# Kernel of six chained blocks on one core: head of the first cross attention, written-out loops and job order of the second one

## The reference

```python
x = x + L0_xattn(layernorm(x), ctx, ctx, wq, bq, wk, bk, wv, bv, wo, bo)  # 16 heads of 8, keys: 1601
x = x + L0_attn(layernorm(x), W_KQV, W_O)                 # causal, rotary, 16 heads of 8
x = x + L0_ffn(layernorm(x), router_w, w1, w2)            # 8 experts, the best 2 used
x = x + L1_xattn(ctx, layernorm(x), ln1.., ln2.., Wq, Wkv, Wo)  # 16 heads of 64, keys: 1601 + 64
x = x + L1_attn(layernorm(x), time_decay, time_first, time_mix, Wk, Wv, Wr, Wo)
x = x + L1_ffn(layernorm(x), w1, b1, w2, b2)              # quantised piecewise-linear GELU
```

## Time and profile before

| | us |
|---|---|
| Median of 3 runs (1848.03 to 1851.46) | 1851.17 |
| The profiled execution, as a run | 1853.56 |
| Its span from first to last instruction | 1851.5 |
| Busy in it: TensorE matmuls (PE) | 1656.6 |
| weight loads (PEld) | 1374.1 |
| VectorE | 1276.0 |
| ScalarE | 959.0 |
| GpSimd | 603.7 |
| First cross attention | until about 570 |
| Second cross attention | about 765 to 1765 |

### The profile page before, as it was taken

One profiled execution on the slowest core, in us unless ns is written; L12 is line 12 of the kernel. 1 busy time (PEld: TensorE's weight loads), 2 busy tenths in 40 slices (PEclk: granted clock), 3 DMA queues, 4 the chain that ended last, 5 costly groups with the idle time before them and its releaser, 6 DMA issues. The chain is left out here.

```text
span 1851.5 us, 36685 instructions
## 1 busy us (share of the span) xinstructions
PE 1656.6 (89%) x13452; PEld 1374.1 (74%) x13452; DVE 1276.0 (69%) x2833; ACT 959.0 (52%) x1788; POOL 603.7 (33%) x855
## 2 busy tenths in 40 slices
PE   6999999999998898289999998999999989999965
PEld 3666666666666787278988888888888888898843
DVE  7666666666673776477777676777776767776577
ACT  3555555655553344155555465555554555556433
POOL 2000000000001221354455545553555455643110
PEclk8999999999998999699999999999999999999986
DMA  5533453535320011300000000000000000000000
GB/s 147 144 72 90 107 145 93 115 90 123 75 55 1 24 47 69 126 30 12 31 19 31 21 22 20 30 30 14 19 31 30 13 20 30 30 1 1 1 3 9
DMA packets 32711, 91.19 MB, mean 49 GB/s; under 512 B 8552, under 2 KB 17424, under 8 KB 32528
## 3 DMA queue, kind: packets, MB, share of 16 engines
q1 hardware_dynamic: 32384, 88.09, 17.7%
q10 hardware_dynamic: 144, 0.61, 0.2%
HBM read 40.43 MB, written 8.91 MB: 27 GB/s over the span
## 5 line engine op out<-in xcount | busy, mean ns | idle before, releaser
L385 DVE TENSOR_TENSOR c_p_lo<-c_turn_ps,c_p_hi 128x512 fp32r<-128x512 f32 x384 | 265.2, 691 | 214.1 <-ACT c_p_hi L334 200.0
L334 ACT ACTIVATE c_p_hi<-c_turn_ps 128x512 fp32r<-128x512 f32 x384 | 228.8, 596 | 296.7 <-PE c_turn_ps L242 292.6
L1006 DVE TENSOR_REDUCE a_chunk_max<-a_side_ps 128x1 f32<-128x512 f32 (+1 forms) x416 | 260.8, 665 | 111.8 <-PE a_side_ps L757 111.6
L376 DVE TENSOR_REDUCE c_chunk_max<-c_score_ps 128x1 f32<-128x1024 f32 (+2 forms) x384 | 262.2, 729 | 31.5 <-PE c_score_ps L272 30.9
L2326 PE MATMUL c_pv_ps<-c_p_hi,c_v_lo 128*128 128x256 f32 (+2 forms) x896 | 267.4, 298 | 0.0
L352 ACT ACTIVATE c_prob<-c_score_ps,c_neg_max 128x1024 f32<-128x1024 f32 (+1 forms) x256 | 245.5, 959 | 39.6 <-DVE c_neg_max L423 39.6
L242 PE MATMUL c_turn_ps<-consts,c_prob 128*128 128x128 f32 (+1 forms) x1792 | 248.7, 278 | 12.7 <-DVE c_p_lo L385 12.4
L2327 PE MATMUL c_pv_ps<-c_p_hi,c_v_hi 128*128 128x256 f32 (+2 forms) x896 | 249.7, 279 | 0.0
L2328 PE MATMUL c_pv_ps<-c_p_lo,c_v_hi 128*128 128x256 f32 (+2 forms) x896 | 249.2, 278 | 0.0
L914 ACT ACTIVATE a_prob<-a_st_ps 128x1024 f32<-128x1024 f32 (+1 forms) x224 | 214.4, 958 | 53.6 <-PE a_st_ps L741 53.6
L242 PEld LDWEIGHTS c_turn_ps<-consts,c_prob 128*128 128x128 f32 (+1 forms) x1792 | 197.4, 141 | 27.2 <-DVE c_p_lo L385 15.3
(11 more groups left out here) (334 smaller groups left out, 2780.5 us busy)
## 6 DMA issues: line engine op xcount, KB each, us to landing
a_stack<-a_k_hi SPq DMA_DIRECT2D x126, 200.1 KB, 4.2
a_stack<-a_k_lo SPq DMA_DIRECT2D x63, 200.1 KB, 4.2
a_ctx<-in_ctx_dram SPq DMA_DIRECT2D x16, 768.0 KB
c_ctx<-in_ctx_dram SPq DMA_DIRECT2D x16, 768.0 KB
absorbed_queries<-b_q_out SPq DMA_DIRECT2D x16, 512.0 KB, 3.5
c_q_raw<-absorbed_queries SPq DMA_DIRECT2D x16, 512.0 KB, 3.2
w<-in_L_ffn_w_dram SPq DMA_DIRECT2D x2, 512.0 KB
fold_raw<-in_L_xattn_Wkv_dram SPq DMA_DIRECT2D x2, 512.0 KB
```

The lines of the kernel that those rows point to most:

```text
L334: last = nc.scalar.activation(p_hi[u][:, 4 * c:4 * c + 4, P * j:P * j + P], turn_ps[c % 2][:].rearrange("p (t q) -> p t q", t=4), ACT.Copy)
L376: nc.vector.reduce_max(chunk_max[:, s % 2, c:c + 1], score_ps[:, maxima_of[c]], AX_X).then_inc(chunk_max_done, 1)
L385: last = nc.vector.tensor_tensor(p_lo[u][part], turn_ps[c % 2][:].rearrange("p (t q) -> p t q", t=4), p_hi[u][part].bitcast(F32), ALU.subt ...
L1006: nc.vector.reduce_max(out, rows, AX_X).then_inc(side_taken, 1)
```

## The change

It has four parts.

1. The `Fori` over passes 1 to 6 of `attend` becomes a Python loop on all five engines, so all eight passes are written out and their semaphore counts are constants.
2. In `attend`, ScalarE does a job "a" ahead of high halves 2 and 3 of its slot, and VectorE does the job "a" of the slot before ahead of low halves 2 and 3.
3. In the first cross attention VectorE splits the late queries an octet after the product: the high part in step 4 and the low part in step 5 of octets 2, 4, 6, 8.
4. In its head, SyncE issues all twelve stacking transfers of batch 0, the high parts as soon as the high keys are there, and ScalarE none. The second `take_turned` comes after the second of the four query splits. The masks of `wo_half` come after the first shift. The first six maxima of octet 1 leave `first_sides`; steps 0 to 3 of octet 0 now hold units 0 to 3, 4 to 7, 8 to 11 and 12.

```diff
@@ attend @@
-        for kind, ks in (("first", 0), ("mid", None)):
-            if ks is None:
-                with sp.Fori(1, BODIES - 1) as k:
-                    lay.sync_body(sp, k, kind)
-            else:
-                lay.sync_body(sp, ks, kind)
+        lay.sync_body(sp, 0, "first")
+        for k in range(1, BODIES - 1):
+            lay.sync_body(sp, k, "mid")
...
-        with pe.Fori(1, BODIES - 1) as k:
+        for k in range(1, BODIES - 1):
             body(k, "mid")
...
+                at(k, kind, s, "a")
                 if before:
                     high_halves(k, kind, s, 2)
                     high_halves(k, kind, s, 3)
-                at(k, kind, s, "a")
...
+                if s and (s - 1, "a") in table[kind]:
+                    lay.dve_take(dve, table[kind][s - 1, "a"], base(kind, k), k, kind, s - 1)
                 if s >= 2 or kind != "first":
                     low_halves(k, s - 1, 2)
                     low_halves(k, s - 1, 3)
                 maximum(k, s, 0)
-                if s and (s - 1, "a") in table[kind]:
-                    lay.dve_take(dve, table[kind][s - 1, "a"], base(kind, k), k, kind, s - 1)
                 maximum(k, s, 1)
@@ first cross attention @@
 def max_units_at(n, s):
+    if n == 0 and s <= 3:
+        return [("max", 1, i) for i in range(4 * s, min(4 * s + 4, UNITS))]
...
-    return [("max", 0, i) for i in range(UNITS)] + [("shift", 0)] + [("max", 1, i) for i in range(6)]
+    return [("max", 0, i) for i in range(UNITS)] + [("shift", 0)]
...
+            def stack_first_keys():
+                sp.wait_ge(k_high, CHUNKS)
+                sp.wait_ge(pads_set, 1)
+                for group in range(2):
+                    stack_part(0, group, 0)
+                    stack_part(0, group, 2)
+                wait_keys_done(sp, 0)
+                for group in range(2):
+                    stack_part(0, group, 1)
+                stack_keys(0, 1)
...
-            act.wait_ge(first_low[0], CHUNKS)
-            for i, part in enumerate((k_hi, k_lo, k_hi)):
-                nc.scalar.dma_start(stack[32 * i:32 * i + 32, 0, 1, 0:CTX].bitcast(F32), part[32:64, :].bitcast(F32)).then_inc(stacked[0], 16)
...
             for i in range(GROUPS):
                 dve.wait_ge(q_done, i + 1)
                 split_queries(i)
-            take_turned(1)
+                if i == 1:
+                    take_turned(1)
             dve.wait_ge(weights_loaded, N_WEIGHTS)
             nc.vector.tensor_copy(bv_wide[:], bv_rows[:].unsqueeze(2).broadcast_to([P, QUADS, P])).then_inc(bias_wide, 1)
-            for i in range(2):
-                nc.vector.tensor_scalar(g.wo_half[:, :, i, :], ...
...
             take_side(sides[UNITS])
+            for i in range(2):
+                nc.vector.tensor_scalar(g.wo_half[:, :, i, :], ...
...
-                    take_queries(job_at(n, s))
+                    if n in (2, 4, 6, 8) and s == 4:
+                        dve.wait_ge(job_taken, number["q", n // 2 - 1, 0] + 1)
+                        high_queries(GROUPS + n // 2 - 1)
+                    if n in (2, 4, 6, 8) and s == 5:
+                        low_queries(GROUPS + n // 2 - 1)
```

More of the change, by code:

```diff
@@ L215, in _ @@
         body(0, "first")
-        with pool.Fori(1, BODIES - 1) as k:
+        for k in range(1, BODIES - 1):
             body(k, "mid")
@@ L364, in _ @@
         body(0, "first")
-        with act.Fori(1, BODIES - 1) as k:
+        for k in range(1, BODIES - 1):
             body(k, "mid")
@@ L442, in _ @@
         body(0, "first")
-        with dve.Fori(1, BODIES - 1) as k:
+        for k in range(1, BODIES - 1):
             body(k, "mid")
@@ L639, in load_ctx, with stack_part @@
                              dram.ctx[b:b + 1, FULL * P:CTX, :].rearrange("o p d -> p (o d)")).then_inc(ctx_loaded, 16)
+            def stack_part(b, group, i):
+                part = (k_hi, k_lo, k_hi)[i]
+                sp.dma_start(stack[32 * i:32 * i + 32, b % 2, group, 0:CTX].bitcast(F32), part[32 * group:32 * group + 32, :].bitcast(F32)).then_inc(stacked[group // 2], 16)
             def stack_keys(b, u):
                 for group in (2 * u, 2 * u + 1):
-                    if b == 0 and group == 1:
-                        continue
-                    for i, part in enumerate((k_hi, k_lo, k_hi)):
-                        sp.dma_start(stack[32 * i:32 * i + 32, b % 2, group, 0:CTX].bitcast(F32), part[32 * group:32 * group + 32, :].bitcast(F32)).then_inc(stacked[u], 16)
+                    for i in range(3):
+                        stack_part(b, group, i)
+            def stack_first_keys():
[8 more added lines that the diff above has]
+                stack_keys(0, 1)
             sp.dma_start(g.x_tok[:], dram.x.rearrange("(t b) s d -> (b s) t d", b=2)).then_inc(loaded, 16)
@@ L670, in _ @@
                     load_ctx(b + 1)
+                if b == 0:
+                    stack_first_keys()
+                    continue
                 wait_keys_done(sp, b)
                 for u in range(QUADS):
-                    if b == 0 and u == 0:
-                        sp.wait_ge(pads_set, 1)
                     if b >= 2:
@@ L1030, in take_keys, with high_queries, low_queries @@
                                                ALU.add, ALU.subtract).then_inc(job_taken, 1)
-            def take_queries(job):
-                if not job or job[0] != "q":
-                    return
-                dve.wait_ge(job_taken, number[job] + 1)
-                split_queries(GROUPS + job[1])
+            def high_queries(i):
+                v, cols = i % GROUPS, slice(i // GROUPS * BANK, i // GROUPS * BANK + BANK)
+                nc.vector.tensor_copy(q_st[:, v, cols].bitcast(F32R), q_raw[i % 2][:]).then_inc(q_high, 1)
+            def low_queries(i):
+                v, cols = i % GROUPS, slice(i // GROUPS * BANK, i // GROUPS * BANK + BANK)
+                dve.wait_ge(q_high, i + 1)
+                nc.vector.tensor_tensor(q_st[64:ONES_AT, v, cols], q_raw[i % 2][64:ONES_AT], q_st[64:ONES_AT, v, cols],
+                                        ALU.subtract).then_inc(q_split, 1)
             def take_low_keys(b, c, bank):
@@ L1052, in split_queries @@
             def split_queries(i):
[L1053 to L1057 removed]
+                high_queries(i)
+                low_queries(i)
             sides = first_sides()
```

10 lines of the change are left out of this document (2 added, 8 removed).

## The result

| | before | after |
|---|---|---|
| Median, us | 1850.65 (4 runs, 1848.03 to 1851.46) | 1797.9 (4 runs, 1797.4 to 1799.11) |
| Ratio to before, 95% interval | | 0.9705 (0.9688 to 0.9723) |
| Profiled execution, us | 1853.56 | 1797.4 |
| Its span, us | 1851.5 | 1795.5 |

The change takes 52.75 us off the median.

The account below looks back on a forecast made before the run. TensorE, busy 1656.6 of 1851.5 us, was taken as the bound, so only its idle gaps and half-clock stretches could go: 26.4 + 17.4 + 7.1 + 6 = 56.9 us off 1851.2, giving 1794; own range 1786 to 1801, 8-in-10 range 1783 to 1809.

Parts of the forecast that it names:

- the list of signs: What would show the forecast in the profile, among it second-attention passes 115 to 116 us long instead of 122.8.
- (c): Second attention: the 3.6 us gaps are work at the turn of a pair and stay; 1820 us, chance 0.06.
- (d): Second attention: straight code waits at each block of code; gain eaten, or up to 1967 us, chance 0.03.
- rival (e): Full clock through the head, and register waits saved in six passes: 1786 us, at the edge of the forecast's 0.62.
- 20.6 - 1.4 = 19.2 us can go: Second attention: all TensorE waits on `c_x_lo` vanish except one of 1.4 us in the preparation.
- rival (a): Second attention, slots 5 and 13: VectorE becomes the limit; 1803 us if half returns, 1811 if all, chance 0.15.
- the margin of 0.6 us: Second attention, slot 5: low half 1 is done some 0.6 us before TensorE's earlier turn 3 needs it.
- The charge of 0.25 us at slot 11: Second attention: half 2 comes later where VectorE has no slack, costing 0.25 us a pass, 7 times, 1.8 us.
- the 1.20 us of the earlier trace: First attention, octets 1, 3, 5, 7: TensorE's side-product wait of 1.20 us goes four times, 4.8 us.
- The charge of 0.2 us for the moved work: First attention: moved VectorE query work only partly fits the spare time, costing 0.2 us for each of four, 0.8.
- The bounds 2 and 9: Head of the first attention: gain 2 us if half clock covers the steps, 9 if it stays away; 6 taken.
- rival (b): Head and late queries give nothing, as TensorE meets key transfers or colder clock: 13.1 us less, 1807 us, chance 0.12.

Follow-up runs that it names:

- c_diag: The changed kernel with GpSimd's diagonal built between the third and fourth normed chunk, run beside the changed kernel on one chip: 1787.57 us, ratio to before 0.9655.
- c_after: The changed kernel as it is, run once more on one chip beside the one with the diagonal moved: 1796.44 us, ratio to before 0.9702.
- b_sides: The changed kernel with the six first maxima of octet 1 back ahead of the first scores: 1804.19 us in one run.
- b_act_issue: The changed kernel with three of the twelve stacking transfers of batch 0 issued by ScalarE again, ahead of the first query copy: 1801.58 us in one run.

## Why the prediction was right, and where its terms were off

The forecast was 1794 us, the measurement 1797.9, inside both ranges. The sum was 56.9 and the profiles differ by 56.0, but that is better than its terms were: two came out 3 to 5 us larger and two 2.5 to 5.5 us smaller, and that they cancelled is luck. The largest piece of the 3.9 us between forecast and median is no term at all: the sum was read from an execution of 1853.56 us and taken off a median of 1851.17, which is 2.4 us. The pass of 122.8 us in the list of signs is 123.0 by the prediction's own rows.

**Part 1, right in mechanism, too small in size.** Forecast 26.4; the loops alone gave 31.1 by points and 29.4 us in the median. The gaps were TensorE's own jump (its loop alone gives 23.5 us), the clock stayed full without them, and straight code had no wait, so rivals (c) and (d) fall. Missing in the sum was what rival (e) had as an extra: the passes without a loop's registers are cheaper, 0.6 us in each. The other 1.5 us of the 31.1 are the half clock at the end of the last pass, which is not the loops'.

**Part 2, over-sized: 17.4 forecast, 12.0 by points (43.1 - 31.1), 11.1 us in the median.** All steady waits on `c_x_lo` went. The step that failed is "20.6 - 1.4 = 19.2 us can go": it took the end of the wait for TensorE's gain in both slots. In slot 5 it was: rival (a), VectorE taking over at turn 3, did not come, so the margin of 0.6 us that I had called the thinnest held. In slot 13 TensorE came 1.3 us earlier to the `norm` product, and there stood 1.06 us for GpSimd. The prediction had not asked what else the next use of the bank needs; it looked at VectorE alone. Moving the diagonal gives the waits back, 8.9 us, which is more than the difference. The charge of 0.25 us at slot 11 failed as well: the wait is 0.75 us after (at 969.09) where the earlier trace rows have 0.92, and it is 0.75 with the loops alone; with the order alone it stayed at 0.93. The pass shows the sum of all: 117.75 us before without its jump, 117.16 with straight loops, 115.65 after, 114.52 in c_diag. The forecast said 115 to 116.

**Part 3, too small: 7.1 forecast, 10.4 by points (7.6 us in the median, with the late queries alone).** The intervals are equal, as forecast, but 33.3 us and not 34. The failed term is the 1.20 us of the earlier trace rows. The profile prints the idle time before a group; the step itself was longer by more. TensorE in octet 1, before:

```profile
82.02 0.74 PE L741 MATMUL a_st_ps<-a_q_bd,a_stack 100*128 100x256 f32 x4
83.96 1.10 PE L757 MATMUL a_side_ps<-a_stack,a_q_bd 96*128 96x512 f32 x2 [1.20 <-DVE a_chunk_max L1006]
84.99 0.41 PE L790 MATMUL a_pv_ps<-a_prob,a_val 65*17 65x128 f32 x8
```

and the same three groups after:

```profile
78.53 0.74 PE L755 MATMUL a_st_ps<-a_q_bd,a_stack 100*128 100x256 f32 x4
79.10 0.62 PE L771 MATMUL a_side_ps<-a_stack,a_q_bd 96*128 96x512 f32 x2
79.66 0.41 PE L804 MATMUL a_pv_ps<-a_prob,a_val 65*17 65x128 f32 x8
```

From the first to the third group it is 2.97 us before and 1.13 after: 1.84 us, of which the bracket shows 1.20. Some 0.5 us are in the length of the pair, 1.10 for 0.62: its second product waited too, inside the group (it starts 0.60 us behind the first, after 0.23). 4 x 1.84 and the half clock of the earlier trace rows (36.72 - 35.17 = 1.55, twice) are the 10.4 us. The charge of 0.2 us for the moved work was not seen anywhere.

**Part 4, over-sized: 6 forecast, 3.5 in this profile.** ScalarE's copy came at 18.11 for a forecast of 17, the first maximum at 25.40 for 24.3, step 4 at 54.82 for 52. Two sizes were wrong. The start itself came about a microsecond later in this execution: the first query product is at 16.94, in before at 15.76, the earliest of the fourteen executions but one. And a step with four units was counted at 3.2 us and took 4.6 and 4.2, because two side banks cannot hold four products: TensorE waits 0.55 us for VectorE in the middle (46.32). On the other side the masks took 0.62 us and not 2.17. The kernels that have this head put the third key product at 69.34 to 71.32, once at 72.75 (the head alone); those without it at 73.98 to 75.35. The bounds 2 and 9 hold that; alone, where the half clock lay badly, it was worth no measurable time, which was one half of rival (b).

**The rest** lost 1.4 us in the last part of the kernel, whose code is the same: its length is 87.2 us in before, 88.7 after and 86.9 in c_diag. Scatter it is not: the four executions with all four parts and the diagonal in its old place (after, c_after, b_sides, b_act_issue) have 88.3 to 88.7, the ten others 86.9 to 87.2. In the first 14 us of it the granted clock is 0.76 after (1706.84 to 1720.84) and 0.88 in before (1764.29 to 1778.29) and c_diag. What makes half clock longer there is open.

**How the parts add.** In medians: loops 29.4, order 11.1 on top of them, head and late queries 14.6 on top of that. Alone the order gave 8.3, the late queries 7.6 and the head 0.9, so one at a time the four make 46 us and together 55. For the order the cause is shown (longer half clock behind jumps that are gone in the whole). For head and queries it is open: the batch intervals are the same with and without the head, and what was seen to differ is where half clock falls. How much that moves can be read in the piece from the fifth batch to the second attention, which the change hardly touches: it takes 562.5 to 570.8 us in the fourteen executions, 568.0 in that of the head alone.

## What to carry to other kernels

When a wait goes, ask of the next product not only whether the engine just relieved keeps up, but for every operand who makes it and what stands ahead of that on its queue: here GpSimd's diagonal, behind work that nobody needed yet, took back 1.06 of the 1.29 us that the order gave in one slot of two, and moving it brought 8.9 us. A loop whose body keeps TensorE full is worth writing out, and for TensorE first. Size a wait by the distance between the instructions around it, in the step with and the step without it, not by the idle time printed in front: the group's own length holds the rest.

## What the runs showed of the hardware

**A jump back of TensorE costs 3.3 to 3.9 us here.** 3.27 to 3.88 us of standstill in before, 17.8 us in five, and TensorE written out alone ends them. The Trainium skill (Advanced Engine Details and Errata, Control Flow Timing) has about 108 ns for a compare-and-branch; the measurement decides, by a factor of thirty or more.

**A pass in a loop against a pass written out.** 0.6 us in a pass of 117 us, with the same work in the same order. The page counts 36685 instructions in before and 34512 with the loops alone; what is gone is mainly the arithmetic on registers that the counts needed. Whether that arithmetic or the wait on a register costs the time is not shown.

**The length of half clock behind a gap isn't set by the gap.** Over the twelve microseconds behind it, a gap of 3.43 us in before had 0.86 of full clock, one of 3.48 us in the same program place with the order alone 0.77, and one of 3.52 us with the head alone, whose passes are those of before, 1.00 (1022.42 to 1034.42). So the gap alone does not set it, and the code of the pass alone does not either.

**VectorE beside GpSimd.** The same two masks of 128x256 took 2.17 us at 27.50 in before and 0.62 us at 38.98 after. What GpSimd did in before at that time:

```profile
26.40 3.13 POOL L697 TENSOR_TENSOR a_q_bd<-a_q_st,a_block_of 96x512 fp32r<-96x512 f32 x3 [1.80 <-DVE a_q_st L1056]
```

The masks end at 29.67, right behind GpSimd's end at 29.53; after, GpSimd is idle when they run. In all six executions with the masks in the old place each of the two took 1.12 or 1.13 us beside GpSimd, in all eight with the new place 0.34 or 0.35. No run was made for it alone. The Trainium skill (SBUF — State Buffer, SBUF: two separate sides) says that some VectorE operations and GpSimd take turns at one pair of ports, each holding it for a whole instruction; this agrees with the rows.
